# First-layer attention scores from rounded parts, and where GpSimd splits the queries

## The reference, cut to what matters

```python
q = jnp.concatenate([q_nope, q_rope], axis=-1)
k = jnp.concatenate([k_nope, jnp.broadcast_to(k_rope, ...)], axis=-1)
scores = jnp.einsum('bqhd,bkhd->bhqk', q, k) * scale     # 4 x 16 x 256 x 256
probs = jax.nn.softmax(scores, axis=-1)
attn = jnp.einsum('bhqk,bkhd->bqhd', probs, v)
```

## Time and profile before

| | |
|---|---|
| median of 3 runs | 676.48 us (676.19 to 676.9) |
| profiled execution, first to last instruction | 675.4 us |
| PE busy | 654.9 us (97%) |
| DVE busy | 500.7 us (74%) |
| ACT busy | 417.7 us (62%) |
| POOL busy | 298.5 us (44%) |
| DMA | 59.43 MB, mean 88 GB/s |

### The profile page before, as it was taken

One profiled execution on the slowest core, in us unless ns is written; L12 is line 12 of the kernel. 1 busy time (PEld: TensorE's weight loads), 2 busy tenths in 40 slices (PEclk: granted clock), 3 DMA queues, 4 the chain that ended last, 5 costly groups with the idle time before them and its releaser, 6 DMA issues.

```text
span 675.4 us, 13827 instructions
## 1 busy us (share of the span) xinstructions
PE 654.9 (97%) x4756; PEld 573.9 (85%) x4756; DVE 500.7 (74%) x1425; ACT 417.7 (62%) x1084; POOL 298.5 (44%) x301
## 2 busy tenths in 40 slices
PE   5999999999999999999999998999999999999998
PEld 3777888898988899888888865556899999999997
DVE  6797877878778787887698788899577745645444
ACT  3766158888888888888865689998554222222221
POOL 1584146546464646452344418999532800400000
PEclk9999999999999999999999999999999999999999
DMA  8903034535535353444560000301100000000000
GB/s 316 378 5 102 1 112 128 167 116 165 165 112 191 100 180 115 123 129 125 210 257 1 1 1 1 112 1 53 75 1 1 2 17 1 1 16 1 2 16 16
DMA packets 26725, 59.43 MB, mean 88 GB/s; under 512 B 3146, under 2 KB 12748, under 8 KB 26272
## 3 DMA queue, kind: packets, MB, share of 16 engines
q1 hardware_dynamic: 23584, 50.35, 22.0%
q0 software_dynamic: 3072, 8.20, 3.7%
HBM read 48.24 MB, written 10.49 MB: 87 GB/s over the span
## 4 chain that ended last, share of the span: by engine, by line
PE 78%; DVE 10%; ACT 6%; issue 3%; POOL 2%; DMA 0%; ACTq 0%; POOLq 0%; DVEq 0%
PE bank L2292 10%; PE bank L2057 8%; PE bank L1991 7%; PE bank L2048 6%; PE bank L2343 5%; PE bank L2317 5%; PE bank L2077 4%; PE bank L2153 4%; PE bank L2068 4%; PE bank L1998 4%; ACT sb L1214 3%; PE bank L2119 3%; PE bank L2200 3%; PE bank L2359 3%; PE bank L1931 2%
## 5 line engine op out<-in xcount | busy, mean ns | idle before, releaser
L1073 ACT ACTIVATE sb<-bank,sb 128x256 f32<-128x256 f32 x128 | 59.6, 472 | 38.7 <-DVE sb L1578 33.5
L1281 ACT ACTIVATE h_parts<-sb 128x256 fp32r<-128x256 f32 x56 | 23.4, 418 | 76.5 <-DVE sb L1836 45.7
L2057 PE MATMUL bank<-sb 128*128 128x256 f32 x256 | 66.2, 381 | 0.0
L1578 DVE TENSOR_REDUCE sb<-bank 128x2 f32<-128x512 f32 x64 | 43.7, 683 | 27.1 <-PE bank L2057 26.6
L2292 PE MATMUL bank<-rounded,b_lo 128*128 128x256 f32 x224 | 63.0, 281 | 0.0
L2292 PE MATMUL bank<-rounded,b_hi 128*128 128x256 f32 x224 | 63.0, 281 | 0.0
L2292 PE MATMUL bank<-am_lo,b_hi 128*128 128x256 f32 x224 | 62.9, 281 | 0.0
L840 POOL DMA_INDIRECT expert_out<-sb x32 | 33.1, 1034 | 58.0 <-DVE sb L1520 44.2
L1080 ACT ACTIVATE sb<-sb 128x256 f32<-128x256 f32 x128 | 57.8, 505 | 0.1
L1827 DVE TENSOR_TENSOR sb<-sb,bank 128x256 f32<-128x256 f32 x56 | 23.4, 419 | 44.6 <-ACT sb L1238 44.5
L1238 ACT ACTIVATE sb<-bank 128x256 f32<-128x256 f32 x56 | 21.4, 382 | 53.3 <-PE bank L2292 53.3
(11 more groups left out here) (321 smaller groups left out, 1950.0 us busy)
## 6 DMA issues: line engine op xcount, KB each, us to landing
sb<-in_w_gate_up SPq DMA_DIRECT2D x32, 368.0 KB
sb<-in_w_down SPq DMA_DIRECT2D x32, 256.0 KB
sb<-in_w_pair SPq DMA_DIRECT2D x8, 704.0 KB
expert_out<-sb SPq DMA_DIRECT2D x1, 4096.0 KB, 23.5
sb<-expert_out SPq DMA_DIRECT2D x8, 512.0 KB, 6.8
sb<-in_w SPq DMA_DIRECT2D x1, 1792.0 KB, 12.9
sb<-in_b SPq DMA_DIRECT2D x1, 1792.0 KB, 7.4
sb<-in_sw_up SPq DMA_DIRECT2D x1, 1536.0 KB, 9.3
```

The source lines that it names most:

```text
L1073: act.activation(probs[:, u % 4, q, :], bank[3 + u % 2][:, q * S:(q + 1) * S], ACT.Exp, scale=-1.0, bias=row_min[:, u % 4, q:q + 1], accum ...
L1578: dve.tensor_reduce(row_min[:, u % 4, :], bank[3 + u % 2][:, :].rearrange("p (q n) -> p q n", q=QT), AX.X, ALU.min).then_inc(at_min, 1)
L2057: mm = pe.matmul(bank[3 + u % 2][:, q * S:(q + 1) * S], qb[i][:, h, b * S + q * P:b * S + (q + 1) * P], keys[:, h, b * S:(b + 1) * S], sta ...
```

## The change: what it does

1. `scores` makes six fp32r products of 128x256 instead of two fp32 ones: for each half of the queries, high queries by high keys, low queries by high keys, high queries by low keys.
2. The high part of the keys (`keys_hi`) is one more ACT copy per token tile in `latents_copied`. POOL subtracts it from `keys` to get `keys_lo` (`key_halves`, four times, once per batch).
3. `qb` becomes one buffer. POOL's new `query_halves(p, c)` makes the parts of half a pair's queries: two casts and two subtractions of 128x512. It stands in POOL's queue in unit 6 for the next pair's first half and in unit 2 for the present pair's second half.
4. `rotated_queries` moves from units 3 and 5 to units 3 and 6. Its writes into `qb` wait for the parts taken before (`at_parts`).
5. `scores` waits for `at_parts` (and in the first pair for `key_parts`) in place of `at_qe` and `at_qm`.
6. SP waits for the last scores (`at_s`) before it loads the expert results, whose tile now overlaps the parts. Three semaphores are merged into others.

```diff
+LAST_HALF_AT, ROTATE_AT, FIRST_HALF_AT = 2, (3, 6), 6
...
-        qb = [r2.take(2, TOK) for _ in range(2)]
+        qb = r2.take(2, TOK)
+        by_half = [w.rearrange("p (h n) -> p h n", h=2) for w in
+                   (xt_parts[:, 0:2 * CH], q_parts1[:, 0:2 * CH], q_lo0[:, :], q_parts1[:, 2 * CH:4 * CH])]
+        qb_hi, qb_lo = by_half[0:2], by_half[2:4]
+        keys_hi, keys_lo = (w[:, :].rearrange("p (h n) -> p h n", h=2) for w in (keys_hi, keys_lo))
...
+        def parts_of(p, c):
+
+            return 8 * p + 4 * c + 4
...
+            sp.wait_ge(at_s, PAIRS * UNITS)
...
+            def key_halves(b):
+
+                batch = slice(b * S, (b + 1) * S)
+                pool.wait_ge(latT_copied, 4 * QT * (b + 1))
+                pool.tensor_tensor(r(keys_lo[:, :, batch]), keys[:, :, batch], keys_hi[:, :, batch], ALU.subtract)\
+                    .then_inc(key_parts, 1)
+
+            def query_halves(p, c):
+
+                half = slice(c * CH, (c + 1) * CH)
+                pool.wait_ge(at_qe, 6 * p + 3 * c + 3)
+                pool.wait_ge(at_qm, 2 * p + c + 1)
+                at_least(pool, at_s, UNITS * (p - 1 + c) + (UNITS // 2 if c == 0 else 0))
+                for h in range(2):
+                    pool.tensor_copy(r(qb_hi[c][:, h, :]), qb[:, h, half]).then_inc(at_parts, 1)
+                for h in range(2):
+                    pool.wait_ge(at_parts, parts_of(p, c) - 3 + h)
+                    pool.tensor_tensor(r(qb_lo[c][:, h, :]), qb[:, h, half], qb_hi[c][:, h, :], ALU.subtract)\
+                        .then_inc(at_parts, 1)
+
-            def rotated_queries(p, c, i):
+            def rotated_queries(p, c):
...
-                at_least(pool, at_s, UNITS * (p - 1))
+                pool.wait_ge(at_parts, parts_of(p - 1, c))
                 pool.wait_ge(at_qe, 6 * p + 3 * c + 1)
...
+            for b in range(2):
+                key_halves(b)
             for p in range(2):
                 split_rope(p, 0)
+                key_halves(2 + p)
+            pool.wait_ge(sh_mm, 2 * NF)
+            pool.wait_ge(latT_mm, NT)
+            query_halves(0, 0)
             pool.wait_ge(rows_out_done, 32)
-            pool.wait_ge(sh_mm, 2 * NF)
             pool.wait_ge(rt_dest, 3)
...
                 for u in range(UNITS):
-                    if u in (3, 5) and p + 1 < PAIRS:
+                    if u == LAST_HALF_AT:
+                        query_halves(p, 1)
+                    if u == FIRST_HALF_AT and p + 1 < PAIRS:
+                        query_halves(p + 1, 0)
+                    if u in ROTATE_AT and p + 1 < PAIRS:
                         transfers_landed(gathers, stores)
-                        rotated_queries(p + 1, (u - 3) // 2, (p + 1) % 2)
+                        rotated_queries(p + 1, ROTATE_AT.index(u))
...
             def latents_copied(i):
+                act.wait_ge(x2_done, NT)
...
+                act.activation(r(keys_hi[:, :, cols]), src[:, 1:3, :], ACT.Copy).then_inc(latT_copied, 1)
                 act.activation(keys[:, :, cols], src[:, 1:3, :], ACT.Copy).then_inc(latT_copied, 1)
...
-                at_least(act, at_s, UNITS * (p - 1))
+                if p:
+                    act.wait_ge(at_parts, parts_of(p - 1, c))
...
-            def scores(g, p, u, i):
+            def scores(g, p, u):
                 b, h = u // 2, u % 2
-                pe.wait_ge(at_qe, 6 * p + 3 * (b // 2) + 3)
-                pe.wait_ge(at_qm, 2 * p + b // 2 + 1)
+                c, batch = b // 2, slice(b * S, (b + 1) * S)
+                pe.wait_ge(at_parts, parts_of(p, c))
+                if p == 0:
+                    pe.wait_ge(key_parts, b + 1)
                 at_least(pe, at_exp, 2 * g - 2)
                 for q in range(QT):
-                    mm = pe.matmul(bank[3 + u % 2][:, q * S:(q + 1) * S],
-                                   qb[i][:, h, b * S + q * P:b * S + (q + 1) * P], keys[:, h, b * S:(b + 1) * S],
-                                   start=True, stop=True)
+                    at = b % 2 * S + q * P
+                    q_hi_, q_lo_ = (w[c][:, h, at:at + P] for w in (qb_hi, qb_lo))
+                    terms = ((q_hi_, keys_hi), (q_lo_, keys_hi), (q_hi_, keys_lo))
+                    for n, (x, k) in enumerate(terms):
+                        mm = pe.matmul(bank[3 + u % 2][:, q * S:(q + 1) * S], r(x), r(k[:, h, batch]),
+                                       start=(n == 0), stop=(n == len(terms) - 1))
                 mm.then_inc(at_s, 1)
```

More of the change, by code:

```diff
@@ L332, in program @@
             end = 0
+            keys_hi = over("keys_hi", start[0], 2 * TOK)
+            q_parts1 = over("q_parts1", start[0] + 2 * NT * D, 2 * 2 * CH)
+            q_lo0 = over("q_lo0", start[1] + 2 * TOK, 2 * CH)
+            keys_lo = over("keys_lo", start[3] + KEYS_AT, 2 * TOK)
+        with ExitStack() as overlay:
+            end = 0
             su_lo = over("su_lo", start[1] + SU_AT, KD * 2 * NF * P)
@@ L574, in program @@
         cf_in, rows_in, proj_in = (sem(n) for n in ("cf_in", "rows_in", "proj_in"))
-        shared_in, zero_set = (sem(n) for n in ("shared_in", "zero_set"))
+        shared_in, pool_first = (sem(n) for n in ("shared_in", "pool_first"))
         ln_stats, ln_mv, ln_var, ln_sd, ln_rstd = (sem(n) for n in ("ln_stats", "ln_mv", "ln_var", "ln_sd", "ln_rstd"))
@@ L604, in program @@
         at_v, at_lo, at_cl = sem("at_v"), sem("at_lo"), sem("at_cl")
+        at_parts, key_parts = sem("at_parts"), sem("key_parts")
         op_mm, op_add = sem("op_mm"), sem("op_add")
@@ L614, in program @@
         b13_split, am_split = sem("b13_split"), sem("am_split")
-        fill_mm, fill_out, step_mask, low_rank = (sem(n) for n in ("fill_mm", "fill_out", "step_mask", "low_rank"))
+        fill_mm, fill_out, low_rank = (sem(n) for n in ("fill_mm", "fill_out", "low_rank"))
         bl_q, bl_bias, bl_s, bl_min, bl_exp, bl_inv, bl_t, bl_even, bl_odd, bl_v, bl_oT, bl_turn, bl_o = (
@@ L1094, in copy_probsT, with merged_queries @@
                                ACT.Copy).then_inc(at_tout, 1)
-            def merged_queries(p, c, i, where):
+            def merged_queries(p, c, where):
                 half = slice(c * CH, (c + 1) * CH)
                 act.wait_ge(at_q, 4 * p + 2 * c + 2)
-                at_least(act, at_s, UNITS * (p - 1))
-                act.activation(qb[i][0:KVL, 0, half], where[0:KVL, :], ACT.Copy, scale=Q_SCALE)
-                act.activation(qb[i][KVL:P, 1, half], where[KVL:P, :], ACT.Copy, scale=Q_SCALE).then_inc(at_qm, 1)
+                if p:
+                    act.wait_ge(at_parts, parts_of(p - 1, c))
+                act.activation(qb[0:KVL, 0, half], where[0:KVL, :], ACT.Copy, scale=Q_SCALE)
+                act.activation(qb[KVL:P, 1, half], where[KVL:P, :], ACT.Copy, scale=Q_SCALE).then_inc(at_qm, 1)
             for c in range(2):
-                merged_queries(0, c, 0, bank[5])
+                merged_queries(0, c, bank[5])
             for p in range(PAIRS):
@@ L1630, in first_queries @@
                 dve.wait_ge(at_qe, 3 * c + 1)
[L1631 to L1632 removed]
+                dve.tensor_tensor(qb[DR:P, 0, half], q_plain[DR:P], q_turned[DR:P], ALU.add).then_inc(at_qe, 1)
+                dve.tensor_tensor(qb[0:DR, 1, half], q_plain[0:DR], q_turned[0:DR], ALU.add).then_inc(at_qe, 1)
             for i in range(NT):
@@ L2084, in pair @@
                     g = UNITS * p + u
-                    scores(g, p, u, i)
+                    scores(g, p, u)
                     experts(p, u, 0)
```

35 lines of the change are left out of this document (17 added, 18 removed).

## The result

| | before | after |
|---|---|---|
| median | 676.69 us (4 runs, 676.19 to 677.38) | 680.71 us (4 runs, 679.98 to 683.49) |
| profiled execution, span | 676.48, 675.4 us | 680.39, 678.6 us |

The ratio is 1.0060, 95% interval 1.0048 to 1.0072: the change costs 4.0 us. The forecast was 676.2, a change of -0.3.

The account below looks back on a forecast made before the run. PE bounds the kernel, then POOL's queue at the present pair length; second to sixth pair 0.0, first 0.0, seventh -1.1, last +0.6, start +0.2 sum to -0.3 us: 676.2 us, range 668.5 to 682.

Parts of the forecast that it names:

- The start, +0.2: Before the first scores: POOL's parts are hidden; the first added ACT copy of the keys costs 0.2 us, bounded 0 to 1.
- line 819's 1.976 us: Mean time of a 128x512 product on POOL, cited as a sign that POOL can be stretched; at its price near 694.
- The first pair, 0.0: First pair: POOL's queue lets PE start the next pair at 115.3 where it started at 115.35, so 0.0.
- POOL's turn of 30.6 us: Pairs: one turn of POOL's queue sums to 30.6 us against 30.57 for the pair before, so POOL fills up.
- rival B: POOL's queue before each pair's first scores: query_halves is the bound and longer than 3.60 us; 682 us; chance 0.18.
- The spacing of 5.12: POOL's transfers in the pairs: the fourth starts 5.12 us after the first, read as the transfers' own spacing.
- rival A: POOL's transfers: the fourth can start 4.04 us after the first, POOL's turn is 28.4, PE bounds; 669 us; chance 0.27.
- PE as the next bound at 29.3: Pairs: the new scores save PE 0.16 us a unit, 1.3 a pair; with PE as bound a pair lasts 29.3.
- the forecast 0.0: Second to sixth pair: PE's saving turns into one wait of some 1.3 us per pair for at_parts; 5 x 0.0.
- Seventh pair, -1.1: Seventh pair, without split_rope: POOL's turn is 29.0 and PE's 29.1, parts just fit; -1.1 us.
- Last pair, +0.6: Last pair: PE waits 1.35 us for expert 29's gather, half of the 1.3 saved on scores given back; +0.6.
- C, the change does nothing on PE: PE's scores: six short products cost as much as the two before, POOL-bound pairs stay; 678 us; chance 0.08.

Follow-up runs that it names:

- e5: Edit of e1: low parts of the third and fourth key batches made behind the first two gathers instead of behind the two split_rope; 678.47 us, 1.0009.
- e3: Changed kernel with the low parts of keys and queries left out; PE multiplies the high parts three times; 673.59 us, 0.9947.
- e2: As e1, and GpSimd's wait for the routing's slots stands ahead of the first query_halves instead of behind it; 681.85 us, 1.0063.
- e7: Edit of e3: PE makes one product of the high parts instead of three; 665.70 us, 0.9820.
- e9: Edit of e5: in the first and last pair ScalarE makes the queries' high parts, GpSimd only the low ones; 675.34 us, 0.9979.
- e10: Edit of e9: ScalarE makes the queries' high parts in all eight pairs; 677.18 us, 1.0002.
- e4: Changed kernel with scores as one fp32 product of the high parts again, low parts made but unused; 683.71 us, 1.0097.
- e11: Edit of e9: GpSimd waits for the routing's slots and issues the first gather before the first low parts of the queries; 680.43 us, 1.0049.
- e6: Changed kernel with the last pair's second-half rotation moved from the seventh pair's unit 6 to the last pair's unit 2; 684.65 us, 1.0101.
- e1: Changed kernel, but GpSimd waits for the routing weights before making the low parts of the first two key batches; 681.13 us, 1.0056.

## Why the prediction was wrong

**The start, +0.2 against +2.31: the step that failed.** The prediction said that `key_halves` and the first `query_halves` "fall into the time before 88.5 us" and "need only be done by the first scores". It asked whether GpSimd had time, not what VectorE did at the same moment. It had the rule on the two engines at hand and applied it to the pairs alone, where VectorE reads PSUM; at the start much of its work is on SBUF alone, and line 819's 1.976 us, all before 60 us, was the sign. What the runs show in its place is a VectorE operation of 0.18 us held for 2.27, and 2.07 us of waiting on PE. e5 shows it: the keys moved away from VectorE's work bring the first scores 2.5 us forward and give 0.5% in time, with every added ScalarE copy in place. For those copies the sum had 0.2 us; e3 and e5 start at 88.17 and 88.31, before the 88.53 of the kernel before, so no run shows a cost.

**The first pair, 0.0 against +1.38.** Same cause, second place. VectorE's slot operations were held (1.28 and 1.16 us), and the first gather starts at 90.64, 0.2 us before the first scores, where it stood 2.4 before them. PE then waits for rows, for VectorE's rounding and for the expert's copy. Without low parts (e3) the pair lasts 26.56; with the slots unheld (e2) 27.49. What each of these waits is worth was not taken apart further.

**POOL's turn of 30.6 us: wrong.** The parts cost what was said, 3.62 us (145.12 to 148.72, and 0.02 to the next), so rival B is out. The spacing of 5.12 was a wait for PE, so rival A was right about it. The prediction set the releaser aside because in rows 5 and 6 "what it waited for" differed; it did not, both rows name PE's line 1991, and only the idle time differs. But A's 29.3 us a pair did not follow, because the other half of both sums was wrong:

**PE as the next bound at 29.3: wrong.** From the scores to the next product a pair's units save 0.08 us four times, 0.12 once and 0.15 three times, not 0.16 throughout: 0.9 us, not 1.3. And of what is saved, the experts' ring through VectorE and ScalarE takes back the two stretches that were already at its length, 7.8 and 6.07 us, and from unit 3 to 5 little is left either (e7). What can be gained is 0.35 us a pair (e3), and the changed kernel got 0.25: its third and fourth pair, 30.61 and 30.46, each lose by late gathers. That the five pairs came out at -1.23, within 1.3 us of the forecast 0.0, is luck: a saving put too high and a wait that did not come cancelled. Rows 2 said "busy 30.57 of 30.57" and I took it for a PE that nothing holds up.

**Seventh pair, -1.1 against -0.53:** e3's 29.86 shows it at the same floor. **Last pair, +0.6 against +1.19:** the mechanism was right, the size off (its own terms, 1.35 less half of 1.3, give 0.7). The gather started 5.84 us after the pair's start where I had 6.0, but took 3.8 us to PE's turn, not 3.0, so the wait was 2.15 us and not 1.35. Its place in GpSimd's queue is one cause: e9 takes the casts, 1.2 us each time, off that queue, the gather starts at 4.8 us, and the wait is gone. The way from issue to landing is the other: e10 has the same casts off the queue, but the rotation stands 0.44 us for an earlier gather's landing, the gather starts at 5.25 us, PE's turn comes 3.65 after it, and 1.07 us of the wait are back. A wait of that length can also be followed by a fall of the clock (e5). One of the four executions of the changed kernel has a mean clock of 0.995, and it is the one of 683.49 us; it has no trace, so where the clock fell is not known.

**C, the change does nothing on PE:** out by e4.

So the loss of 4.0 us was on the record as a way to be wrong ("if the start costs more than 1 us"), but not as a rival with a price. The range held 680.71, which is no merit of the sum: it had 0.2 us at the start, where most of the loss lies, and its sign had the wrong side as likeliest.

## What to carry to other kernels

Work that an idle engine takes over is not free because the engine is idle: look at what runs beside it. GpSimd arithmetic on SBUF belongs beside VectorE operations that read PSUM, not beside comparisons and products on SBUF alone on which a chain hangs, however short they are. And before a saving on the fullest engine is counted, measure the loop between two like events on it, here one expert's product to the next; where it keeps its length with less work in it, another engine sets it, though the busy column says 100%. And look at the mean clocks before comparing two medians: in e2 the median and the executions at full clock point to different sides.

## What the runs showed of the hardware

- A VectorE operation that is held up by GpSimd's arithmetic on SBUF does not slow down in proportion, it stands still until GpSimd is through: 32 columns took 2.27 us beside two subtractions, 1.28 and 1.16 beside one each, and 128x512 took 4.01 us while a gather's issue and two subtractions went by (e11). An operation with an input from PSUM kept its time: line 1701 took 0.49 us at 70.61 beside GpSimd, and 0.48 before. The Trainium skill (SBUF — State Buffer, Terms) describes the port pair that the two engines share as an exclusive lock, held for a whole instruction, under which the loser fully blocks. The traces agree, and show more than one instruction's worth: the loser can lose again to the next GpSimd instruction, 2.27 us against the 1.24 of one subtraction.
- Not every VectorE operation on SBUF alone is held. Just before the held comparison a reduction, line 1531, took the 1.22 us that it takes in the kernel before too, and the reciprocals of the pairs (line 1635, 64 of them, most beside GpSimd) never took more than 0.17. The reduction, and GpSimd at that time:

```profile
58.74 1.22 DVE L1531 TENSOR_REDUCE sb<-sb 128x32 f32<-128x1024 f32 x1
```

```profile
58.49 1.29 POOL L839 TENSOR_TENSOR sb<-sb 64x512 f32<-64x512 f32 x1 [0.46 <-ACT sb L1078]
```

- Held were comparisons with a scalar (1533, 1553) and operations with two inputs from SBUF (1556, the rotary products). The Trainium skill's rule that the prediction cites (GPSIMD Engine Reference, Specifications) agrees for the two inputs and for the reduction, which has one; the comparisons have one too, and fit only if they ran in the two-port mode, which no row shows. A gather's issue by itself held none of the rotary products that ran within it: 0.69 us at 86.4 in the kernel before, at 90.96 in the changed one and at 90.26 in e11. Why the one at 86.22 in e11 did not get through in the same way is open.
- A wait of PE can be followed by a stretch at the 1.2 GHz level. Four of the thirteen profiled executions have one: it began 1.3 us after PE took up work again behind a wait of 1.51 us (e2) and of 1.92 us (e5), within a wait of 2.40 us (e6), and after waits of 1.43, 2.19 and 0.95 us in a row (e11), and it lasted 3.4 us, in e6 6.8. Behind waits of 2.07 and 2.15 us in the changed kernel, 2.06 in e1, 2.00 in e4 and 1.98 in e2 there was none. Whether it comes differs between executions of one kernel too. Of the twelve executions of e5, seven have a mean clock of 1.00 and take 676.99 to 678.64 us, five have 0.997 and take 678.72 to 679.95. In e9, without such a wait, all eleven have 0.999 or 1.00.
- Who loses changes from place to place: beside VectorE's rotary products in e2 GpSimd's two subtractions took 3.44 us, not 2.56. In the changed kernel's trace the fourth key subtraction was the one held (2.36 us at 73.99), in e1 VectorE beside it (2.17 us at 72.57). So a fix is read from the next collision, not from the one that it removed.
- Products of 128x256: from the first fp32r product after an fp32 one to the next it takes 0.20 us, from one after another fp32r product 0.12.
